# The causal mask of the narrow score units, moved from a TensorE product to a VectorE addition

## The chip, the cores and the metric

One Trainium2 chip, one of its cores. The metric is the device time of one execution in microseconds. Within the core five engines run from queues of their own: TensorE (PE, with its weight loads shown as PEld), VectorE (DVE), ScalarE (ACT), GpSimd (POOL) and SyncE (SP, which only issues DMAs here). They wait for one another on semaphores. Each queue is worked off strictly in its written order.

## The reference

The kernel computes one transformer layer with adaptive layer norm on x of shape 2 x 1024 x 128, in float32. What matters here is the attention; behind it stand a router with the two best of eight experts for each token and a shared expert.

```python
h = _layernorm(x) * (1 + ca) + sa
c_q, c_kv = h @ W_dq, h @ W_dkv
Q = (c_q @ W_uq).reshape(2, 1024, 16, 8)       # K, V likewise from c_kv
scores = jnp.einsum('bqhd,bkhd->bhqk', Q, K) / math.sqrt(8)
scores = jnp.where(jnp.tril(jnp.ones((1024, 1024), bool)), scores, -jnp.inf)
attn = jax.nn.softmax(scores, axis=-1)
out = jnp.einsum('bhqk,bkhd->bqhd', attn, V).reshape(2, 1024, 128)
x = x + ga * (out @ W_o)
h = _layernorm(x) * (1 + cb) + sb
x = x + gb * (shared_expert(h) + the two best of eight experts, weighted)
```

## The kernel before

Attention runs as eight tasks, t = 0 to 7: two batches by four groups of four heads. A task has two halves of 512 queries (c = 0, 1) and key blocks j of 128 keys. Three kinds of work belong to a task.

*Max units* (`max_scores`, L1598 to 1613, and `max_unit`, L1221 to 1237). For the softmax the kernel first needs each query's largest score. TensorE forms scores of 128 queries against up to 512 keys in one PSUM bank (`mx`), and VectorE reduces them: a plain reduction (L1235) off the diagonal, a masking reduction (L1231, one instruction a head) on it. The results of a half are gathered (`maxima`, negm, L1244), split in three bfloat16 parts by GpSimd, turned by TensorE (L1621), copied by VectorE (`neg_out`, L1252) and sent by DMA into three extra rows of the query operand. The product of a score unit then holds the score minus the maximum already. There are 38 max units in a task. They, and the turned pieces of other stages, take the banks `mx` 0, 1, 2 in turn: TensorE may fill a bank again only when the unit three places earlier has been read (`ring_free`).

*Score units* (`score_unit`, L1624 to 1649). TensorE forms the scores of 128 keys against the queries from the diagonal on, up to 512 columns in a bank (`sc`). SCORE lists the 38 units of a task. Where the queries left of a half are at most 256 wide, a unit packs two heads (256 columns each) or four (128 columns each) in one bank. So the units with more than one head are, in each task, 8, 9 (two heads) and 10 (four heads) of the first half, and 35, 36 (two) and 37 (four) of the second: the last three of each half, one right after the other. All other diagonal units hold one head. On the diagonal (22 of the 38 units) a further product, identity times `after`, adds -3e38 where the key is later than the query (L1646 to 1649); `after` holds four copies of the 128 x 128 triangle in bfloat16, and one product covers the first 128 columns of each head of the unit. ScalarE then takes the exponential of the unit in one instruction (`exps`, L894). The banks `sc` 0, 1, 2 go round too: score unit g waits for the exponential of unit g - 3 (four banks near the end of the last task).

*Weighing* (`weigh`, L1652 to 1667). TensorE multiplies the exponentials `pr` with the values, four heads side by side on the array, in float32, into `oacc`. Weighing of two key blocks at a time (of one in the first and last task) is placed when the score units are three units past them (LAG; four in the last task). At the end of a half ScalarE copies `oacc` out (L903), TensorE turns it (L1674) and VectorE divides (L1267, L1269).

The order is written out by `attention_order`, and all engines walk the same list. Max units run ahead of the score units: at first 20, then three for each of the first ten score units, and from there one max unit after each score unit, so that score unit k of task t is followed by max unit k + 2 of task t + 1. After the last max unit of a half its turning is due five max units later. `BETWEEN` and `LATE` put other work into the list: the gates (VectorE L1114 to 1126) in task 1, the row modulations in task 3, the projection and the routing of finished tokens in tasks 4, 5 and 7, and the lists of expert tiles (`tile_list`, L1304 on) at score units 3, 5, 7, 9 of task 7. VectorE has in this list the max units, the copies and the routing, but no work on score units. The experts follow the attention and begin when all weighing is done (`up_copy`, L1350).

The lines which the change touches:

```python
act.wait_ge(s["score_ready"], g + 1)                       # exps
elif kind == "score" and t == T - 1 and k in FIRST_LIST:   # VectorE's walk
if diagonal:                                               # score_unit
```

Of the kernel before, what the change touches and what calls it, by code (L numbers as in the profile page):

```python
# [13 lines left out]
ALU = mybir.AluOpType  # L14
# [7 lines left out]
P = 128  # L22
# [41 lines left out]
SCORE = score_units()  # L64
NM = len(MAXU)
NU = len(SCORE)
# [33 lines left out]
FIRST_LIST = (3, 5, 7, 9)  # L100
# [100 lines left out]
    return held, prior, turned, lent  # L201


def span(g, h):

    return (4 * g + 2 * h, 2) if g == 3 else (4 * g, 4)


def adaln_layer(nc, x, cT, wmod, wdqT, wdkvT, wuq, wuk, wuv, wo, wr1, br1, wr2, br2,
# [18 lines left out]
    for kind, t, k in ORDER:  # L228
        if kind == "out" and k == 0:
            task = t  # L230
        elif (kind, t, k) in SPARE_BANK:
            LENT[kind, t, k] = task
            BACK[task + 1] = (kind, t, k)
    FREED = {x: n + 1 for units in (BY_ACT, BY_DVE) for n, x in enumerate(units)}
    DIAGONAL = [(t, k) for t in range(T) for k in range(NM) if MAXU[k][6]]
    RING = 3
    NLOAD = 9
# [10 lines left out]
    with ExitStack() as ctx:  # L248
# [3 lines left out]
        def sem(name):  # L252
# [139 lines left out]
            xt_ready xt_done up_w down_w hid_ready y_done  # L392
            const_ready pad_ready chain_v chain_p chain_a cs_ready csb_ready comp_ready wqkv_ready mod_ready mod_done r1b_ready ones_ready
            var_ready std_ready xn_ready xT_ready hT_ready qk_ready hi_ready r1_ready mid_ready lo_ready
            v_ready v_done aux_ready aux_free negm_ready neg3_ready score_ready exp_done
            vb_ready pv_done o_done var2_ready
            xn2_ready gx_ready up_ready dn_ready acc_done y_ready wog_ready
            act_free rowm_ready gs_ready""".split()
# [413 lines left out]
        def _(act):  # L812
# [71 lines left out]
            def exps(t, k):  # L884

                c, j, h, n, q0, w, _ = SCORE[k]
                g = NU * t + k
                group = NG * t + GROUPS.index((c, j))
                if h == 0 and group >= NBUF:
                    act.wait_ge(s["pv_done"], group - NBUF + 1)  # L890
                act.wait_ge(s["score_ready"], g + 1)
                src = score_bank(g)[:, 0:n * w].rearrange("p (h n) -> p h n", h=n)
                at = q0 - HALF * c
                act.activation(pr[:, group % NBUF, h:h + n, at:at + w], src, ACT.Exp,  # L894
                               scale=float(DK) ** -0.5).then_inc(s["exp_done"], 1)
# [127 lines left out]
        def _(dve):  # L1023
# [197 lines left out]
            def max_unit(t, k, a):  # L1221
# [14 lines left out]
                        "p (h n) -> p h n", h=n), AX_X, ALU.max)  # L1236
                ins.then_inc(s["aux_free"], 1)

            def maxima(t, c):

                dve.wait_ge(*freed(("max", t, LAST_MAX[c])))
                if t >= 1:
                    dve.wait_ge(s["neg3_ready"], 2 * t + c - 1)
                dve.tensor_reduce(negm[:, c, :], mxp[:, c, :, :, :].rearrange("p k h i -> p (h i) k"), AX_X, ALU.max,  # L1244
                                  negate=True).then_inc(s["negm_ready"], 1)
# [138 lines left out]
            for kind, t, k in ORDER:  # L1384
                a = PLACE.get((kind, t, k))
                if (kind, t, k) in ON_ACT:
                    continue
                if kind == "max":
                    max_unit(t, k, a)
                    if k in LAST_MAX:  # L1390
                        maxima(t, LAST_MAX.index(k))
                    for g, step in norms:
                        if step < 2:
                            second_stats(g, step)
                        else:
                            second_var(g)
                    norms = [(g, step + 1) for g, step in norms if step < 2]
                    for g, step in bests:
                        if step == 0:
                            best_two(g)  # L1400
                        elif step < 3:
                            best_index(g, step - 1)
                        else:
                            choose(g)
                    bests = [(g, step + 1) for g, step in bests if step < 3]
                elif kind == "turn":
                    neg_out(t, k, a)
                elif kind == "mod":
                    mod_out(a)
                elif kind == "gates":  # L1410
                    gates_out(a)
                elif kind == "rowmod":
                    rowmod_out(a)
                elif kind == "at":
                    attn_turned(t, a)
                elif kind == "wo":
                    second_x(t, k, a)
                    if t < 2:
                        norms.append((t, 0))
                    elif t == 3 and k == 0:  # L1420
                        second_stats(t, 0)
                    elif t == 3:
                        second_stats(t, 1)
                        second_var(t)
                    else:
                        second_stats(t, 0)
                        second_stats(t, 1)
                        second_var(t)
                        second_rstd(t)
                elif kind == "x2t":  # L1430
                    hidden_turned(t, a)
                elif kind == "rt":
                    router_relu(t, k, a)
                elif kind == "lg":
                    logits_out(t, k, a)
                    if t < 2:
                        bests.append((t, 0))
                    elif t == 3:
                        best_two(t, k)
                        best_index(t, k)  # L1440
                    else:
                        best_two(t)
                        best_index(t, 0)
                        best_index(t, 1)
                        choose(t)
                elif kind == "pf":
                    slots_of(t, a)
                elif kind == "list":
                    tile_list(t, k)
                elif kind == "score" and t == T - 1 and k in FIRST_LIST:  # L1450
                    tile_list(0, FIRST_LIST.index(k))
                elif kind == "pick":
                    choose(t)
                elif kind == "root":
                    second_rstd(t, 1 if k else 2)
                elif kind == "begin":
                    experts.append(expert(0))
                    up_copy(0)
                elif kind == "half":
                    half_out(k, a)  # L1460
                elif kind == "first":
                    experts.append(expert(1))
                    up_copy(1)
                    down_copy(0)
                elif kind == "out":
                    attn_out(t, k, a)
                elif kind == "head":
                    if t + 2 < ROUTED:
                        experts.append(expert(t + 2))
                        up_copy(t + 2)  # L1470
                    if t + 1 < ROUTED:
                        down_copy(t + 1)
                elif kind == "down" and k == 3:
                    shared_out(t, a)
                elif kind == "odds":
                    gate_sums()
                elif kind == "tail":
                    y_out(t)
# [24 lines left out]
        def _(pe):  # L1503
# [120 lines left out]
            def score_unit(t, k):  # L1624
# [15 lines left out]
                for m in range(n):  # L1640
# [2 lines left out]
                    ins = pe.matmul(dst[:, w * m:w * m + w], S3[0:CROSS + 3, r3, 0, kk:kk + P],  # L1643
                                    S3[0:CROSS + 3, r3, 1, q:q + w], start=(m == 0), stop=True,
                                    skip_group_check=(m > 0))
                if diagonal:  # L1646

                    ins = pe.matmul(dst[:, 0:n * w].rearrange("p (h n) -> p h n", h=n)[:, :, 0:P], identb[:, :],  # L1648
                                    after[:, 0:n, :], start=False, stop=True, skip_group_check=True)
# [260 lines left out]
```

## Time and profile before

| | |
|---|---|
| time, median of 3 runs | 447.58 us (446.93 to 448.43) |
| span of the profiled execution | 445.2 us |
| PE busy | 397.4 us, 89% |
| PE weight loads busy | 231.8 us, 52% |
| DVE busy | 326.0 us, 73% |
| ACT busy | 265.9 us, 60% |
| POOL busy | 142.9 us, 32% |
| mean granted TensorE clock | 0.969 of full speed |

The page gives no time for the profiled execution beside its span; the span is 2.4 us less than the median. Attention's score units lie between 46 and 308 us, the experts between 309 and 421 us. Two things must be kept in mind in reading a timeline. A matmul's duration includes its way through the array, and the next one starts before it ends: what it costs in a row of matmuls is the distance from its start to the next start. The same holds, in a smaller measure, for VectorE, where a reduction's record lasts 0.68 us and the next begins after 0.61 us.

### The profile page before, as it was taken

To read this page: it belongs to the slowest core of one execution; us is meant where nothing else is said; L and a number is where in the kernel's file an instruction comes from. 1 tells how busy PE (TensorE), PEld (TensorE's weight loads), DVE (VectorE), ACT (ScalarE), POOL (GpSimd) and SP (SyncE) were. 2 spreads that over 40 slices of the span, in tenths; PEclk is the share of its full clock that TensorE was granted. 3 is DMA by queue.
4 is the path that set the end of the run, shared out by engine and by line. 5 is a ranking of instruction groups with operands and counts; after the bars stand their busy time and mean duration, and the time that the engine had idled before them with its cause. 6 is when DMAs were issued, how large, how long until landed. Compare 5 with 4: busy or idle time off the path is not lost.

```text
span 445.2 us, 9323 instructions
## 1 busy us (share of the span) xinstructions
PE 397.4 (89%) x2901; PEld 231.8 (52%) x2901; DVE 326.0 (73%) x1187; ACT 265.9 (60%) x609; POOL 142.9 (32%) x237
## 2 busy tenths in 40 slices
PE   6679889989999999999989899999989999999900
PEld 3335433443443543545533443434767889999900
DVE  5747799888888887889796887735687665555527
ACT  3623647647666766667665566787756755555632
POOL 2520350000010020105576333504177575334410
PEclk9959999999999999999999999999999999999975
DMA  5433321044040120210210000493012233210153
GB/s 151 144 112 109 94 58 54 1 104 148 1 110 1 35 77 0 67 45 0 68 45 18 21 21 18 116 315 70 7 54 67 73 91 95 68 36 27 37 194 102
DMA packets 28819, 31.77 MB, mean 71 GB/s; under 512 B 4851, under 2 KB 23387, under 8 KB 28267
## 3 DMA queue, kind: packets, MB, share of 16 engines
q1 hardware_dynamic: 26067, 26.12, 21.1%
q0 software_dynamic: 2272, 4.67, 3.1%
q8 instruction: 23, 0.38, 0.4%
q10 hardware_dynamic: 432, 0.39, 0.3%
q14 instruction: 25, 0.20, 0.2%
HBM read 21.04 MB, written 9.85 MB: 69 GB/s over the span
## 4 chain that ended last, share of the span: by engine, by line
PE 69%; DVE 14%; issue 5%; DMA 5%; ACT 3%; POOL 2%; SPq 1%; DVEq 0%; ACTq 0%; POOLq 0%
PE oacc L1665 14%; PE mx L1612 12%; PE sc L1643 11%; PE sc L1798 6%; PE oacc L1811 6%; DVE mxp L1235 3%; DVE masked L1231 3%; PE sc L1648 2%; PE sc L1818 2%; PE mx L1765 2%; PE mx L1674 2%; ACT osb L903 2%; POOL slot_rows L734 2%; PE mx L1754 1%; DMA parts<-token_results 1%
## 5 line engine op out<-in xcount | busy, mean ns | idle before, releaser
L894 ACT ACTIVATE pr<-sc 128x512 f32<-128x512 f32 (+1 forms) x296 | 154.0, 579 | 87.3 <-PE sc L1648 47.6
L1612 PE MATMUL mx<-S 72*128 72x512 bf16 (+3 forms) x384 | 112.8, 331 | 13.6 <-DMA S<-q_parts 6.1
L1231 DVE CUSTOM_DVE_ANT_0 masked<-mx,later 128x128 f32<-128x128 f32 (+3 forms) x256 | 111.6, 485 | 17.0 <-PE mx L1612 16.1
L1643 PE MATMUL sc<-S 75*128 75x512 bf16 (+3 forms) x373 | 108.1, 328 | 0.0
L1235 DVE TENSOR_REDUCE mxp<-mx 128x1 f32<-128x512 f32 x128 | 82.5, 684 | 20.9 <-PE mx L1612 20.5
L1665 PE MATMUL oacc<-pr,vb 128*32 128x512 f32 (+3 forms) x768 | 73.9, 493 | 0.0
L1612 PEld LDWEIGHTS mx<-S 72*128 72x128 bf16 x384 | 34.7, 99 | 52.2 <-DVE mxp L1231 14.8
L958 ACT ACTIVATE pr<-sc,bcur 128x128 f32<-128x128 f32 x156 | 44.6, 369 | 26.6 <-PE sc L1798 26.5
L1643 PEld LDWEIGHTS sc<-S 75*128 75x128 bf16 x373 | 34.5, 97 | 46.4 <-issue 21.2
L740 POOL DMA_INDIRECT token_results<-S,xrow x39 | 39.1, 1003 | 48.0 <-DVE S L1372 44.6
L654 POOL CAST neg<-negm 128x16 bf16<-128x16 f32 x16 | 3.2, 198 | 139.7 <-DVE negm L1244 139.7
L1798 PE MATMUL sc<-xTg,vb 128*128 128x128 f32 x312 | 41.6, 276 | 2.6 <-ACT xTg L950 2.5
L1811 PEld LDWEIGHTS oacc<-vb,pr 128*128 128x128 f32 x312 | 39.0, 192 | 7.2 <-issue 6.0
L1648 PE MATMUL sc<-after,identb 128*128 128x128 bf16 (+2 forms) x172 | 41.9, 244 | 0.0
L1811 PE MATMUL oacc<-vb,pr 128*128 128x128 f32 x312 | 41.3, 275 | 0.3 <-ACT pr L958 0.3
L734 POOL DMA_INDIRECT slot_rows<-parts,rowi x32 | 31.6, 986 | 30.2 <-PE sc L1648 13.6
L1798 PEld LDWEIGHTS sc<-xTg,vb 128*128 128x128 f32 x312 | 37.9, 192 | 3.6 <-ACT xTg L950 3.3
L1665 PEld LDWEIGHTS oacc<-pr,vb 128*32 128x32 f32 x768 | 19.0, 108 | 31.1 <-issue 15.9
L1357 DVE COPY vb<-S 128x512 f32 x39 | 18.4, 472 | 20.8 <-issue 11.3
L1372 DVE TENSOR_TENSOR S<-oacc,be_sb 128x128 f32<-128x128 f32 x39 | 11.3, 290 | 18.0 <-PE oacc L1811 16.4
L1231 DVE DVE_READ_ACCUMULATOR2_ANT mxp<- 128x1 f32 x256 | 21.0, 82 | 0.0
L1648 PEld LDWEIGHTS sc<-after,identb 128*128 128x128 bf16 x172 | 16.8, 98 | 7.4
(279 smaller groups left out, 471.2 us busy)
## 6 DMA issues: line engine op xcount, KB each, us to landing
S<-q_parts SPq DMA_DIRECT2D x48, 96.0 KB
S<-k_parts SPq DMA_DIRECT2D x21, 192.0 KB
xrow<-slot_rows SPq DMA_DIRECT2D x39, 64.5 KB, 1.8
S<-in_we SPq DMA_DIRECT2D x1, 2048.0 KB, 9.1
S<-in_we SPq DMA_DIRECT2D x4, 512.0 KB, 9.9
parts<-token_results SPq DMA_DIRECT2D x4, 512.0 KB, 5.7
x_sb<-in_x SPq DMA_DIRECT2D x4, 256.0 KB, 4.0
out_y<-attn SPq DMA_DIRECT2D x4, 256.0 KB, 2.3
```

What stands on the lines that cost most here:

```text
L734: pool.indirect_dma_start(xd, bass.IndirectOffsetOnAxis(ap=rowi[:, g, k, n:n + 1], axis=0), rowsk[:, g % 2, n, k, :], None).then_inc(sent[ ...
L740: pool.indirect_dma_start(yd, bass.IndirectOffsetOnAxis(ap=xrow[:, i % XR, C:C + 1].bitcast(I32), axis=0), yst[:, i % ROWS, :], None).then ...
L894: act.activation(pr[:, group % NBUF, h:h + n, at:at + w], src, ACT.Exp, scale=float(DK) ** -0.5).then_inc(s["exp_done"], 1)
L958: ins = act.activation(hid[:, i % 2, P * f:P * f + P], sc[:, i % 2, P * f:P * f + P], ACT.Silu, bias=bcur[:, i % FREE, f:f + 1])
L1231: ins = dve.tensor_tensor_reduce(masked[:, d % 2, w * m:w * m + w], unit[a][:, w * m:w * m + w], later[:, HALF - w:HALF], 1.0, LOWEST, ALU ...
L1235: ins = dve.tensor_reduce(mxp[:, c, place, h:h + n, i - 4 * c], unit[a][:, 0:n * w].rearrange("p (h n) -> p h n", h=n), AX_X, ALU.max)
L1612: ins = pe.matmul(dst[:, w * m:w * m + w], S3[0:CROSS, r3, 1, q:q + P], S3[0:CROSS, r3, 0, kk:kk + w], start=(m == 0), stop=True, skip_gro ...
L1643: ins = pe.matmul(dst[:, w * m:w * m + w], S3[0:CROSS + 3, r3, 0, kk:kk + P], S3[0:CROSS + 3, r3, 1, q:q + w], start=(m == 0), stop=True, ...
L1648: ins = pe.matmul(dst[:, 0:n * w].rearrange("p (h n) -> p h n", h=n)[:, :, 0:P], identb[:, :], after[:, 0:n, :], start=False, stop=True, s ...
L1665: ins = pe.matmul(oacc[VW * h:VW * h + VW, c, at:HALF], vb[:, t % 2, j, h, :], pr[:, group % NBUF, h, at:HALF], start=(j == 0), stop=(j == ...
L1798: ins = pe.matmul(sc[:, i % 2, P * f:P * f + P], wcur[:, i % 2, P * f:P * f + P], xTg[:, i % 2, :], start=True, stop=True)
L1811: ins = pe.matmul(oacc[:, i % 2, 0:P], hid[:, i % 2, P * f:P * f + P], wcur[:, i % 2, FF + C * f:FF + C * f + C], start=(f == 0), stop=(f ...
```

## The change

A new helper names the units: task 1 or later, diagonal, more than one head. These are six units in each of seven tasks, 42 in all. For them TensorE leaves its mask product out and signals after the score products. VectorE, at the unit's place in the common list (before the max unit that follows it there, and before a piece of `tile_list`), waits for the signal and adds `after` in place to the first 128 columns of each head (`blot`), and ScalarE's exponential waits for that addition instead of the product. The semaphore `blot_done` counts the additions. Everything else, task 0 included, stays.

```diff
+def masked_by_dve(t, k):
+    return t >= 1 and SCORE[k][6] and SCORE[k][3] > 1
...
+    BLOTTED = [(t, k) for t in range(T) for k in range(NU) if masked_by_dve(t, k)]
...
     # ScalarE, exps
-                act.wait_ge(s["score_ready"], g + 1)
+                if masked_by_dve(t, k):
+                    act.wait_ge(s["blot_done"], BLOTTED.index((t, k)) + 1)
+                else:
+                    act.wait_ge(s["score_ready"], g + 1)
...
     # VectorE
+            def blot(t, k):
+                _, _, _, n, _, w, _ = SCORE[k]
+                g = NU * t + k
+                dve.wait_ge(s["score_ready"], g + 1)
+                corner = score_bank(g)[:, 0:n * w].rearrange("p (h n) -> p h n", h=n)[:, :, 0:P]
+                dve.tensor_tensor(corner, corner, after[:, 0:n, :], ALU.add).then_inc(s["blot_done"], 1)
...
-                elif kind == "score" and t == T - 1 and k in FIRST_LIST:
-                    tile_list(0, FIRST_LIST.index(k))
+                elif kind == "score":
+                    if masked_by_dve(t, k):
+                        blot(t, k)
+                    if t == T - 1 and k in FIRST_LIST:
+                        tile_list(0, FIRST_LIST.index(k))
...
     # TensorE, score_unit
-                if diagonal:
+                if diagonal and not masked_by_dve(t, k):
```

## Rows read from the trace of the kernel before

**Rows 1.** The page: busy time by engine, then the chain that ended last.

```profile
PE 397.4 (89%) x2901; PEld 231.8 (52%) x2901; DVE 326.0 (73%) x1187; ACT 265.9 (60%) x609; POOL 142.9 (32%) x237
...
PE 69%; DVE 14%; issue 5%; DMA 5%; ACT 3%; POOL 2%; SPq 1%; DVEq 0%; ACTq 0%; POOLq 0%
```

**Rows 2.** Windows: stretch, its length, then busy PE, PEld, DVE, ACT, POOL.

```profile
100.00:280.00 180.00, 173.51 (x1311) 79.82 (x1310) 151.21 (x552) 118.19 (x232) 47.84 (x108) 1.00 0.15 42
```

**Rows 3.** Groups by line and shape: busy us, mean ns, idle before.

```profile
L1149 DVE TENSOR_TENSOR x_sb<-oacc,x_sb 128x512 f32<-128x512 f32 x2 | 1.4, 688 | 0.0
L1149 DVE TENSOR_TENSOR x_sb<-mx,x_sb 128x256 f32<-128x256 f32 x2 | 0.8, 408 | 0.0
```

**Rows 4.** Timeline of PE, task 3, end of the second half: start, us, instruction.

```profile
178.53 0.38 PE L1648 MATMUL sc<-after,identb 128*128 128x512 bf16 x1
178.75 0.38 PE L1612 MATMUL mx<-S 72*128 72x256 bf16 x2
...
182.25 0.34 PE L1612 MATMUL mx<-S 72*128 72x384 bf16 x1
```

**Rows 5.** Timeline of DVE, the same stretch, with idle time before in brackets.

```profile
178.54 0.69 DVE L1231 CUSTOM_DVE_ANT_0 masked<-mx,later 128x512 f32<-128x512 f32 x1
...
181.41 0.42 DVE L1231 CUSTOM_DVE_ANT_0 masked<-mx,later 128x256 f32<-128x256 f32 x1 [0.40 <-PE mx L1612]
...
183.95 0.56 DVE L1231 CUSTOM_DVE_ANT_0 masked<-mx,later 128x384 f32<-128x384 f32 x1 [0.68 <-PE mx L1612]
```

**Rows 6.** Timeline of PE and DVE, task 4, end of the first half.

```profile
186.52 0.27 PE L1648 MATMUL sc<-after,identb 128*128 128x256 bf16 x1
186.63 0.38 PE L1612 MATMUL mx<-S 72*128 72x512 bf16 x1
...
190.44 1.29 DVE L1235 TENSOR_REDUCE mxp<-mx 128x1 f32<-128x512 f32 x2 [1.00 <-PE mx L1612]
...
191.19 0.40 PE L1612 MATMUL mx<-S 72*128 72x128 bf16 x4
```

**Rows 7.** Timeline of PE: its waits for DVE in tasks 1 and 5.

```profile
97.86 0.39 PE L1612 MATMUL mx<-S 72*128 72x512 bf16 x1 [1.23 <-DVE gB L1117]
...
226.81 0.40 PE L1612 MATMUL mx<-S 72*128 72x128 bf16 x4 [0.29 <-DVE mxp L1235]
```

**Rows 8.** Timeline of DVE: idle after the narrow units in tasks 3, 4, 5, 6.

```profile
160.79 1.29 DVE L1235 TENSOR_REDUCE mxp<-mx 128x1 f32<-128x512 f32 x2 [0.70 <-PE mx L1612]
...
214.37 0.42 DVE L1231 CUSTOM_DVE_ANT_0 masked<-mx,later 128x256 f32<-128x256 f32 x1 [0.84 <-PE mx L1612]
...
253.09 0.42 DVE L1231 CUSTOM_DVE_ANT_0 masked<-mx,later 128x256 f32<-128x256 f32 x1 [0.34 <-PE mx L1612]
...
262.79 0.69 DVE L1235 TENSOR_REDUCE mxp<-mx 128x1 f32<-128x512 f32 x1 [0.81 <-PE mx L1612]
```

**Rows 9.** Timeline of PE, DVE and ACT: end of task 6, task 7.

```profile
282.76 0.38 PE L1643 MATMUL sc<-S 75*128 75x512 bf16 x1
...
283.40 0.22 DVE L1252 COPY negT<-mx 48x128 bf16<-48x128 bf16 x1 [1.95 <-PE mx L1621]
...
288.51 0.22 DVE L1326 TENSOR_REDUCE tile_e<-past 128x9 f32<-128x72 f32 x1
...
289.58 0.17 DVE L1332 TENSOR_TENSOR at_e<-at_e,took_e 128x8 f32<-128x8 f32 x1
...
291.05 0.39 PE L1643 MATMUL mx<-S 75*128 75x512 bf16 x1
...
307.28 0.74 DVE L1197 TENSOR_SCALAR parts<-mx,br_sb 32x512 f32<-32x512 f32 x1 [2.15 <-PE mx L1733]
...
307.89 0.60 ACT L894 ACTIVATE pr<-sc 128x512 f32<-128x512 f32 x1 [0.77 <-PE sc L1648]
```

**Rows 10.** Timeline of DVE: the shortest 512 wide operation, and a stretched one.

```profile
95.93 0.43 DVE L1115 TENSOR_SCALAR attn<-attn 128x512 f32<-128x512 f32 x1
...
232.27 1.25 DVE L1296 SCALAR_TENSOR_TENSOR rowi<-place 128x8 int32<-128x8 f32 x1
```

More of the change, by code:

```diff
@@ L394, in adaln_layer @@
             var_ready std_ready xn_ready xT_ready hT_ready qk_ready hi_ready r1_ready mid_ready lo_ready
-            v_ready v_done aux_ready aux_free negm_ready neg3_ready score_ready exp_done
+            v_ready v_done aux_ready aux_free negm_ready neg3_ready score_ready blot_done exp_done
             vb_ready pv_done o_done var2_ready
```

## The prediction

> **What bounds the kernel now.** I read the page first: TensorE is busy for 89% of the span and holds 69% of the chain that ended last, VectorE 14% [rows 1]. Then one row of the windows over 100 to 280 us, six tasks of steady work: PE 173.5 us of 180, DVE 151.2, ACT 118.2 [rows 2]. TensorE is short of time there, and VectorE, idle for 28.8 us, is not far behind. The row hides where that idle time lies, and on this the change depends. So I read the timelines of PE and DVE around the units that the change touches. They come in runs of three: units 8, 9, 10 (call it run A of a task) and 35, 36, 37 (run B), in tasks 1 to 7, so fourteen runs. The reader is to see two things. TensorE's starts follow one another without a gap, so a product taken away is time for it. And at these runs VectorE is behind TensorE: at 178.54 it begins a reduction and works on without a pause until 181.01, and the pause that ends there is 0.40 us [rows 5], while TensorE began its last max unit before the weighing at 178.75 [rows 4]. TensorE's max unit at 182.25 can start only because VectorE has just read the bank of the one begun at 181.41 (0.69 us of work, to 182.10) [rows 4, 5]: there the engine that ends last is VectorE. After a run comes the weighing, some 1.6 us of TensorE without a max unit, in which VectorE catches up and then idles; that pause is what can absorb more work.
>
> **What the change takes off TensorE.** One mask product of a two-head unit costs the distance of two starts, 186.52 to 186.63, 0.11 us; of a four-head unit 178.53 to 178.75, 0.22 us [rows 4, 6]; the records last 0.27 and 0.38 us, which is depth, not cost. A run holds two and one: 0.44 us. Fourteen runs: 6.2 us. The identity's weight loads go too; they lay under the products before.
>
> **What it puts on VectorE.** No row shows an addition that reads and writes PSUM. The nearest are the additions of a PSUM bank to SBUF, 688 ns for 512 columns and 408 ns for 256 [rows 3]. Two 512 wide reductions in a row take 1.29 us where one takes 0.68 [rows 6], so the next starts 0.61 us on, 0.07 to 0.08 less than the record. I take 0.61 and 0.34 us: 1.29, say 1.28 us a run, 17.9 us over fourteen runs. Bounds: below, the 512 wide operation that lasts 0.43 us [rows 10] and half of it for 256, 0.86 us a run; above, a small operation stretched to 1.25 us by something else [rows 10], which, once in a run, makes it 1.9 us. The nearest rows are of the same operation and width, so I stay with them.
>
> By the Trainium skill's page "VectorE: DVE Perf Modes", section on the TRN2 errata, an operation with a PSUM source costs 120 + FD cycles at 0.96 GHz. That is an estimate of 0.66 and 0.39 us, 1.44 us a run, where the rows give 1.28; by the page the total below would be some 2 us higher.
>
> **What waits behind it.** VectorE does the addition in the list's order, so after the max units it is behind with, and on its own queue the next max unit, the negated maxima and the turned pieces stand behind it. ScalarE's exponential of the unit waits for it; TensorE's score unit three later waits for the exponential (0.5 to 0.6 us), and the max unit three later for VectorE. Both reach TensorE.
>
> *Run B, task 3.* Insert 0.34 before the max unit at 178.54, 0.34 before the next, 0.61 before the one after. VectorE's next unit then starts not at 181.41 but at 181.01 + 1.28 = 182.3, 0.88 later, as 0.40 of the 1.28 went into the pause [rows 5]. TensorE's max unit at 182.25 waits for its bank and had some 0.1 of slack: it moves to 183.0, 0.75 later [rows 4]. The other path: the addition of unit 37 ends about 181.5 and its exponential at 182.2, and then the score unit three later can start, ahead of the max unit that VectorE holds until 183.0: this path is just under the first. The 0.44 us that TensorE saves in the run come ahead of both waits and are lost in them. Afterwards VectorE has its pause of 0.68 us at 183.95 again, as both engines are late by the same, so the delay stays and does not grow.
>
> *Run A, task 4.* The pause behind it is 1.00 us [rows 6]. 1.28 less 1.00 leaves 0.28; the max unit at 191.19 has 0.1 of slack: 0.2 us. Again TensorE's 0.44 is spent waiting; the score unit that needs unit 10's exponential comes 0.1 late.
>
> *All runs*, by the same step (1.28 less VectorE's next pause, less 0.1 where TensorE has it):
> - A of tasks 2 and 4: 0.2 each. A3: pause 0.70 [rows 8]: 0.5. A6: pause 0.81 [rows 8]: 0.4.
> - A1 and A5: VectorE works on without a pause on the gates and on the routing, and TensorE already waits for it, 1.23 and 0.29 us [rows 7]. Nothing absorbs: 1.2 each.
> - B1, B2, B3: 0.75 each. B4: pause 0.84: 0.35. B5: pause 0.34: 0.85 [rows 8].
> - B6: no max units are left, VectorE idles 1.95 us before 283.40, from 281.45 [rows 9]. Only the path by the exponentials counts: with the additions VectorE is done with unit 37 at 281.45 + 1.28 = 282.7, the exponential ends 283.3, and the third score unit of task 7 starts then instead of at 282.76 [rows 9]: 0.5 us.
> - A7: unit 9's addition stands before a piece of the tile list and unit 10's behind it; the piece takes 288.51 to 289.75 [rows 9]. With two additions of 0.34 ahead of the piece, unit 10's runs from 290.4 to 291.1, its exponential to 291.7, and the score unit that takes its bank, four on, starts then instead of at 291.05 [rows 9]: 0.7.
> - B7: unit 37's addition stands behind a routing copy that lasts from 307.28 to 308.0, and takes 0.65: the exponential starts at 308.7, not 307.89 [rows 9]. Its weighing is the last of the attention. Some 0.2 of the 0.8 lies under the weighing of the blocks before it, queued ahead: 0.6 (an estimate). The experts start after it.
>
> Sum: runs A 1.2 + 0.2 + 0.5 + 0.2 + 1.2 + 0.4 + 0.7 = 4.4 us; runs B 2.25 + 0.35 + 0.85 + 0.5 + 0.6 = 4.6 us. In all +9.0 us, with TensorE's savings already in it. Attention's end shifts the experts as a whole. Against the span: 445.2 + 9.0 = 454.2. The median of the runs lies 2.4 us above that span, so 447.6 + 9.0 = 456.6 us. With 0.86 us a run instead of 1.28 each run gives some 0.4 less, 3 us after all; with 1.9 some 0.6 more each, 17. The exponential path sets in at 0.86 as well, so the low end is nearer 3 to 4.
>
> **The rivals.**
> *TensorE keeps its gain.* If VectorE's idle time did take all additions (17.9 us against 28.8 us in 180), each run would shorten by 0.44 us: 447.6 - 6.2 = 441.4 us. For it speaks TensorE's share [rows 1, 2]. Against it: the idle time is not at the runs; it decides only where the pause after a run exceeds 1.28 + 0.44, and only B6 has such a one [rows 9], the rest 0.34 to 1.00. A half of it, additions absorbed and TensorE's gain lost, would be no change, 447.6: for that the priced 1.28 would have to be under the pauses, true of none but B6.
> *The exponentials end last and cost more.* Three banks hold the score units. If the hand-over from TensorE to VectorE to ScalarE takes 0.2 us more than the rows of handed-over work show (starts within 0.1 us of the end before), or VectorE's copy of the negated maxima comes late and its DMA holds the next half, each of twelve runs costs some 0.4 more: 447.6 + 9.0 + 5 = 461.6. For it: three hand-overs in a row where there was one. Against: ScalarE is idle for a third of the time [rows 2] and starts at once.
> *A delay is given back in part.* Where TensorE is held by VectorE anyway (A1, A5, B5), a late run can meet slack that I can't see, for instance the 1.25 us operation [rows 10] that runs behind A5 and may not be stretched at another moment. Then 3 to 5 us of the nine remain: 452.
>
> **How the numbers follow.** My forecast, a loss of 7 to 12 us: 0.50. Given back in part, 450 to 454.5: 0.22. Exponentials on top, above 459.5: 0.12. Within 0.3% (about 1.3 us, what a measurement can tell from nothing) of 447.6 or slightly off: 0.07. TensorE keeps a gain: 0.09. Slower by over 0.3%, 0.84; the same 0.07; faster 0.09. The time is 456.6; the range 450.0 to 461.5 leaves the two ends outside.
>
> **What would show each step.** L1648 drops by 42 products; the new addition's line shows 42 instructions, 28 of about 410 and 14 of about 690 ns. In 100 to 280 us and its longer successor DVE busy grows by 15 us and PE's does not fall by as much as its work. VectorE's pauses behind the runs B vanish or shrink to 0.1, PE's waits for `mxp` (weight loads of L1612) grow, and ScalarE waits for the addition. The distance from one run B to the next in tasks 2 and 3 grows by 0.9 to 1.0 us. The stretch after the attention keeps its length. I am wrong if that distance falls, if VectorE's pauses behind the runs stay as they are, or if the additions last well under 0.4 us.

## The result, and the profile after

The changed kernel takes 461.6 us (median) against 448.4 us of the kernel before in the same comparison; the ratio is 1.027, with a 95% interval of 1.023 to 1.031. That is 12.0 us slower (10.3 to 13.7). Forecast were 9.0 us more, 456.6 us, and a range of 450.0 to 461.5. The direction came out, the size was 3 us short, and the median lies 0.1 us above the top of the range; the ratio times the forecast's own base of 447.6 gives 459.6. One of the five executions of the changed kernel, 469.9 us, was in the chip's slower state and is not in the ratio. The profiled execution's span is 457.2 us, 12.0 more than before; its time, 459.0 us, is the lowest of the five.

The page first: busy time, then TensorE's granted clock in forty slices (9 is nine tenths of full speed or more), then the chain that ended last.

```profile
PE 402.4 (88%) x2859; PEld 228.9 (50%) x2859; DVE 342.6 (75%) x1229; ACT 265.6 (58%) x609; POOL 142.7 (31%) x237
...
PEclk9979999989999999999998799999999999999975
...
PE 55%; DVE 24%; issue 9%; DMA 5%; ACT 4%; POOL 2%; SPq 1%; DVEq 1%; ACTq 0%; POOLq 0%
```

The same row of clocks in the kernel before:

```profile
PEclk9959999999999999999999999999999999999975
```

TensorE has 42 products fewer and its share of the chain falls from 69% to 55%; VectorE's rises from 14% to 24% [rows 1]. VectorE is busy for 16.6 us more. One thing the prediction did not have: slices of the attention in which the clock of TensorE is below full speed (the ninth, and the 22nd and 23rd). The groups by line and shape (busy us, mean ns, idle before) give the price of an addition and who waits now:

```profile
L1254 DVE TENSOR_TENSOR sc<-sc,after 128x256 f32<-128x256 f32 x28 | 11.7, 425 | 1.0 <-PE sc L1663 0.9
L1254 DVE TENSOR_TENSOR sc<-sc,after 128x512 f32<-128x512 f32 x13 | 9.0, 689 | 0.0
L903 ACT ACTIVATE pr<-sc 128x512 f32<-128x512 f32 x234 | 126.7, 604 | 90.8 <-DVE sc L1254 41.2 <-PE sc L1663 25.9 <-PE sc L1668 23.2
L1632 PEld LDWEIGHTS mx<-S 72*128 72x128 bf16 x384 | 34.5, 98 | 54.4 <-DVE mxp L1240 17.4 <-DVE mxp L1244 9.2 <-issue 8.5
L1663 PEld LDWEIGHTS sc<-S 75*128 75x128 bf16 x373 | 35.0, 98 | 57.3 <-ACT pr L903 25.9 <-issue 20.0
```

425 and 689 ns are close to what the nearest rows said (408 and 688) [rows 3]. ScalarE waits 41.2 us for the additions, most of it in place of waits for TensorE: in the kernel before its idle time ahead of these exponentials was 78.8 us, here it is 90.8. The distance from one run B to the next, forecast to grow by 0.9 to 1.0 us, grows by 0.91 and 0.93 (marks below). Now the place that the prediction worked out, the end of task 3's second half, by engine, DVE first, then ACT, then PE (start, us, instruction, idle before):

```profile
181.17 0.43 DVE L1254 TENSOR_TENSOR sc<-sc,after 128x256 f32<-128x256 f32 x1
181.51 0.68 DVE L1240 CUSTOM_DVE_ANT_0 masked<-mx,later 128x512 f32<-128x512 f32 x1
...
182.34 0.42 DVE L1254 TENSOR_TENSOR sc<-sc,after 128x256 f32<-128x256 f32 x1
...
183.50 0.69 DVE L1254 TENSOR_TENSOR sc<-sc,after 128x512 f32<-128x512 f32 x1
184.11 0.41 DVE L1240 CUSTOM_DVE_ANT_0 masked<-mx,later 128x256 f32<-128x256 f32 x1
...
187.32 0.56 DVE L1240 CUSTOM_DVE_ANT_0 masked<-mx,later 128x384 f32<-128x384 f32 x1 [0.68 <-PE mx L1632]
```

```profile
184.29 2.07 ACT L903 ACTIVATE pr<-sc 128x512 f32<-128x512 f32 x4 [0.91 <-DVE sc L1254]
```

```profile
184.94 0.39 PE L1663 MATMUL sc<-S 75*128 75x512 bf16 x1 [0.56 <-ACT pr L903]
...
185.62 0.34 PE L1632 MATMUL mx<-S 72*128 72x384 bf16 x1
```

The next instruction starts 0.34 us after an addition of 256 columns begins and 0.61 after one of 512. (From the 120 + FD cycles at 0.96 GHz of the Trainium skill, "VectorE: DVE Perf Modes", section on the TRN2 errata, the estimate is 0.39 and 0.66 us; from start to start the trace has 0.05 less, and it decides.) The pause of 0.40 us [rows 5] is gone, and the one of 0.68 is back unchanged behind the run. TensorE waits 0.56 us for the exponential of unit 37. Behind that the weight load of the max unit at 185.62 waits another 0.20 for VectorE. So here the path by the exponential, which the prediction had just under the other, takes the larger part of the delay.

A good ruler for such a kernel is the row of ScalarE's copies of `oacc` at the end of each half: sixteen marks, found by filtering the timeline of ACT. The marks of tasks 2 and 3 (A2, B2, A3, B3), before and then after:

```profile
133.04 0.59 ACT L903 ACTIVATE osb<-oacc 128x512 f32<-128x512 f32 x1
...
153.74 0.59 ACT L903 ACTIVATE osb<-oacc 128x512 f32<-128x512 f32 x1
...
163.58 0.59 ACT L903 ACTIVATE osb<-oacc 128x512 f32<-128x512 f32 x1
...
184.28 0.59 ACT L903 ACTIVATE osb<-oacc 128x512 f32<-128x512 f32 x1
```

```profile
134.73 0.59 ACT L912 ACTIVATE osb<-oacc 128x512 f32<-128x512 f32 x1
...
156.18 0.59 ACT L912 ACTIVATE osb<-oacc 128x512 f32<-128x512 f32 x1
...
166.21 0.59 ACT L912 ACTIVATE osb<-oacc 128x512 f32<-128x512 f32 x1
...
187.65 0.59 ACT L912 ACTIVATE osb<-oacc 128x512 f32<-128x512 f32 x1
```

The marks are 1.69, 2.44, 2.63 and 3.37 us later. What a mark's delay adds to the delay of the mark before it is its *step*, the cost of one run of three units: 0.75 for B2, 0.19 for A3, 0.74 for B3. Where the clock does nothing they repeat from profile to profile of a kernel within some 0.02 us, far finer than the time of a kernel can be told, and they are the measure in what follows.

### The profile page after: what moved, and what is told of

Same layout as the page of the kernel before. It is cut to its first block, busy times and chain, and to the rows that moved or that the text cites. A ratio compares the mean times of both kernels' runs of the same rounds, so it can differ in the third digit from the quotient of the medians.

```text
span 457.2 us, 9282 instructions
## 1 busy us (share of the span) xinstructions
PE 402.4 (88%) x2859; PEld 228.9 (50%) x2859; DVE 342.6 (75%) x1229; ACT 265.6 (58%) x609; POOL 142.7 (31%) x237
## 4 chain that ended last, share of the span: by engine, by line
PE 55%; DVE 24%; issue 9%; DMA 5%; ACT 4%; POOL 2%; SPq 1%; DVEq 1%; ACTq 0%; POOLq 0%
PE oacc L1685 11%; PE mx L1632 8%; PE sc L1663 8%; DVE masked L1240 7%; PE sc L1818 6%; PE oacc L1831 5%; DVE mxp L1244 3%; DVE sc L1254 3%; PE mx L1785 2%; PE sc L1838 2%; POOL slot_rows L740 2%; ACT pr L903 2%; PE mx L1694 1%; PE mx L1774 1%; ACT osb L912 1%
## 5 line engine op out<-in xcount | busy, mean ns | idle before, releaser
L903 ACT ACTIVATE pr<-sc 128x512 f32<-128x512 f32 (+1 forms) x296 | 154.0, 581 | 99.3 <-DVE sc L1254 41.2
L1632 PE MATMUL mx<-S 72*128 72x512 bf16 (+3 forms) x384 | 113.3, 333 | 14.4 <-DMA S<-q_parts 6.5
L1240 DVE CUSTOM_DVE_ANT_0 masked<-mx,later 128x128 f32<-128x128 f32 (+3 forms) x256 | 112.2, 484 | 14.4 <-PE mx L1632 13.4
L1663 PE MATMUL sc<-S 75*128 75x512 bf16 (+3 forms) x373 | 109.8, 332 | 4.1 <-ACT pr L903 4.0
L1685 PE MATMUL oacc<-pr,vb 128*32 128x512 f32 (+3 forms) x768 | 79.8, 525 | 0.6 <-ACT pr L903 0.6
L1668 PE MATMUL sc<-after,identb 128*128 128x128 bf16 (+2 forms) x131 | 29.3, 224 | 0.0
L1254 DVE TENSOR_TENSOR sc<-sc,after 128x256 f32<-128x256 f32 (+1 forms) x41 | 20.6, 509 | 1.0 <-PE sc L1663 0.9
```

The lines of the kernel that those rows point to most:

```text
L1240: ins = dve.tensor_tensor_reduce(masked[:, d % 2, w * m:w * m + w], unit[a][:, w * m:w * m + w], later[:, HALF - w:HALF], 1.0, LOWEST, ALU ...
L1254: dve.tensor_tensor(corner, corner, after[:, 0:n, :], ALU.add).then_inc(s["blot_done"], 1)
L1632: ins = pe.matmul(dst[:, w * m:w * m + w], S3[0:CROSS, r3, 1, q:q + P], S3[0:CROSS, r3, 0, kk:kk + w], start=(m == 0), stop=True, skip_gro ...
L1685: ins = pe.matmul(oacc[VW * h:VW * h + VW, c, at:HALF], vb[:, t % 2, j, h, :], pr[:, group % NBUF, h, at:HALF], start=(j == 0), stop=(j == ...
```

## The experiments

Three theories. *V*: VectorE's queue ends last at the runs; its additional work reaches TensorE less the next pause. *H*: the hand-over from TensorE to VectorE to ScalarE costs by itself. *C*: TensorE's granted clock falls, and that is the part beyond the forecast. Where three marks are shown, they are B2, A3 and B3 of that profile, to be compared with the steps 0.75, 0.19, 0.74 of the change. Steps are always against the first profile of the kernel before. The experiments ran on several chips: for the first four, and for all from "only the second halves" on, the kernel before took 462.2 us and not 448. Ratios are always against it on the same chip, and the changed kernel itself was not timed where it takes 462.2.

**TensorE keeps its products too.** VectorE adds zeros (`nought`), and the exponential waits for that.

```diff
-                dve.tensor_tensor(corner, corner, after[:, 0:n, :], ALU.add).then_inc(s["blot_done"], 1)
+                dve.tensor_tensor(corner, corner, nought[:, 0:n, :], ALU.add).then_inc(s["blot_done"], 1)
...
-                if diagonal and not masked_by_dve(t, k):
+                if diagonal:
```

> TensorE keeps its mask product in the 42 units, and VectorE still adds a tile of the same size (zeros, so that the score stays what it was) which the exponential waits for. Tells what TensorE's 6.2 us of saved products were worth. Theory V (VectorE's queue ends last at the runs, the saving is lost in its waits): within 0.3% to at most 1.5 us above the changed kernel, so 11 to 14 us over the kernel before. Rival P (the saving was realised and hides a larger loss): 5 to 6 us above the changed kernel, 17 to 18 over before. Theory C (TensorE's granted clock fell because it had less to do): TensorE is busier here, fewer stretches at half clock than the four of the changed kernel, and the time may even be below it.

Ratio 1.020 (1.017 to 1.024) against the kernel before, 9.3 us, under the 11 to 14 expected; as the changed kernel has no time on that chip, the marks decide.

```profile
161.04 0.59 ACT L913 ACTIVATE osb<-oacc 128x512 f32<-128x512 f32 x1
...
171.07 0.59 ACT L913 ACTIVATE osb<-oacc 128x512 f32<-128x512 f32 x1
...
192.52 0.59 ACT L913 ACTIVATE osb<-oacc 128x512 f32<-128x512 f32 x1
```

From mark to mark 10.03 and 21.45 us, as in the changed kernel (10.03 and 21.44), where TensorE does 0.44 us less in each. What TensorE saves is worth nothing in the ordinary tasks (2 and 3, and run A of task 4) while VectorE adds; it is worth 0.1 us in A7 (1.18 here against 1.08) and 0.2 in B7 (0.57 against 0.34). Theory C's guess, that a busier TensorE keeps its clock, fell: over 103 to 119 us the granted clock is 0.68 here, 10 us at the lower level.

**The products left out, no mask at all.** VectorE's additions go too, and the exponential of these units runs on a thousandth of the score so that it stays finite; this kernel leaves the mask out.

```diff
-                if masked_by_dve(t, k):
-                    act.wait_ge(s["blot_done"], BLOTTED.index((t, k)) + 1)
-                else:
-                    act.wait_ge(s["score_ready"], g + 1)
+                act.wait_ge(s["score_ready"], g + 1)
...
-                dve.wait_ge(s["score_ready"], g + 1)
-                corner = score_bank(g)[:, 0:n * w].rearrange("p (h n) -> p h n", h=n)[:, :, 0:P]
-                dve.tensor_tensor(corner, corner, after[:, 0:n, :], ALU.add).then_inc(s["blot_done"], 1)
```

> The 42 mask products are left out and nobody adds the mask (these units are not masked; their exponential runs with a thousandth of the scale so that it stays finite). The most that the change can give. If TensorE ends last at the runs: 5 to 6 us below the kernel before. If VectorE holds TensorE there (theory V): 1 to 3 us below, as only the second pieces without max units and the exponential path gain.

Ratio 0.999 (0.997 to 1.001): no gain that the time shows, less than the 1 to 3 us that theory V expected.

```profile
153.70 0.59 ACT L909 ACTIVATE osb<-oacc 128x512 f32<-128x512 f32 x1
...
163.28 0.59 ACT L909 ACTIVATE osb<-oacc 128x512 f32<-128x512 f32 x1
...
183.92 0.59 ACT L909 ACTIVATE osb<-oacc 128x512 f32<-128x512 f32 x1
```

Steps -0.26 for A3 (-0.36 for A2 and A4) and -0.06 for B2 and B3. In the second halves of tasks 1 to 3 six sevenths of TensorE's 0.44 us are lost even without any addition, as VectorE ends last there anyway; in the first halves of tasks 2 to 4 most of it is won, and in A7 and B7, with -0.44 each, all of it. From A1 to B4 this is 1.35 us. Behind it this profile, of an execution of 468.6 us, lies at half clock in tasks 5 and 6 (steps B5 5.60, A6 3.91) and loses it all again.

**Load alone.** VectorE adds from SBUF to SBUF, for nobody, and waits for nothing but its own addition before; TensorE masks, ScalarE waits for TensorE.

```diff
-                dve.wait_ge(s["score_ready"], g + 1)
-                corner = score_bank(g)[:, 0:n * w].rearrange("p (h n) -> p h n", h=n)[:, :, 0:P]
-                dve.tensor_tensor(corner, corner, after[:, 0:n, :], ALU.add).then_inc(s["blot_done"], 1)
+                if (t, k) != BLOTTED[0]:
+                    dve.wait_ge(s["blot_done"], BLOTTED.index((t, k)))
+                dve.tensor_tensor(idle[:, :].bitcast(BF16)[:, 0:n * P], later[:, 0:n * P],
+                                  after[:, 0:n, :].rearrange("p h n -> p (h n)"), ALU.add).then_inc(s["blot_done"], 1)
```

> As the kernel before, TensorE masks, the exponential waits for TensorE; but VectorE does 42 additions of the same width at the same places of its queue, from SBUF to SBUF, for which nobody waits. Theory V: 5 to 9 us over the kernel before, most of the loss. Theory H (the hand-over TensorE to VectorE to ScalarE makes it): under 2 us over.

Ratio 1.017 (1.013 to 1.022).

```profile
162.44 0.59 ACT L909 ACTIVATE osb<-oacc 128x512 f32<-128x512 f32 x1
...
172.48 0.59 ACT L909 ACTIVATE osb<-oacc 128x512 f32<-128x512 f32 x1
...
193.95 0.59 ACT L909 ACTIVATE osb<-oacc 128x512 f32<-128x512 f32 x1
```

Steps 0.77, 0.20 and 0.77. The load by itself makes the whole step of the ordinary tasks, and the additions' content, their PSUM bank and the saved products make none. It does not make the steps of B4 (0.01), A7 (0.00) and B7 (-0.06), and of B6 only 0.43.

**Hand-over alone.** TensorE masks; ScalarE waits for a count of VectorE, which waits for the unit and does nothing else.

```diff
-                dve.tensor_tensor(corner, corner, after[:, 0:n, :], ALU.add).then_inc(s["blot_done"], 1)
+                dve.sem_inc(s["blot_done"], 1)
```

> As the kernel before, TensorE masks; but the exponential of the 42 units waits for a semaphore that VectorE counts up at the unit's place in its queue, after it waited for the score unit, without any addition. Theory H: 4 us or more over the kernel before. Theory V: under 2 us over: the wait in VectorE's order costs only where VectorE is far behind (first run of task 1, task 5).

Ratio 1.008 (1.005 to 1.010), 3.6 us.

```profile
155.58 0.59 ACT L912 ACTIVATE osb<-oacc 128x512 f32<-128x512 f32 x1
...
165.42 0.59 ACT L912 ACTIVATE osb<-oacc 128x512 f32<-128x512 f32 x1
...
186.12 0.59 ACT L912 ACTIVATE osb<-oacc 128x512 f32<-128x512 f32 x1
```

Steps 0.00, 0.00, 0.00, and in all tasks only A5 0.42 and A7 0.32, the two places where small routing operations stand in VectorE's queue, and B5 3.25, of which more below. So V, and not H. The time lies between what the two theories expected (under 2 us, 4 or more) and does not tell them apart: 1.8 us were lost before the first hand-over and some behind the attention, so they are no effect of the hand-over that I can show.

**The kernel before again, on a chip on which it takes 447.8 us.**

> The kernel before, unchanged, for its profile on the chip of this call: a chip on which it took 462.2 us was met in the call before, against 447.6 on the chip of the first comparison. Theory C (TensorE's granted clock makes the difference between chips and between runs): more stretches at half clock than the one at 21 to 31 us that the first profile of it has, where the time is above 450. If the time is 447 to 450, no further stretch.

It ran once, in 449.0 us; its span is 447.3, 2.1 more than the first profile's. Busy time and clock of the stretch of task 5, first profile, then this one (PE, PEld, DVE, ACT, POOL, clock):

```profile
228.00:256.00 28.00, 24.58 (x180) 10.86 (x181) 21.81 (x88) 16.32 (x32) 15.86 (x22) 1.00 0.05 16
```

```profile
228.00:256.00 28.00, 25.30 (x145) 10.54 (x144) 19.28 (x75) 14.30 (x28) 14.04 (x19) 0.82 0.04 14
```

Theory C's bound was wrong: at 449 us the kernel before has time at half clock too, by the clock of 0.82 some 10 us of the 28. Its step B5 is 3.46 us with no addition anywhere. The first profile, on which the prediction rested, was one without it.

**The changed kernel again.**

> The changed kernel, unchanged, on the same chip as the others of this call. Theory V with the sum of the prediction (9.0 us): ratio 1.020. Theory C on top, as in the first profile (17 us at half clock within the attention): ratio 1.025 to 1.03, and its profile has more time at half clock within the attention than the kernel before on this chip.

Four times between 457.9 and 473.1 us against 447.8, too far apart for a ratio. Steps of its profile: A1 2.14 and B1 5.78, and then 0.17, 0.75, 0.19, 0.75, 0.17, 0.60 up to B4, the same as in the first but for A1 and B1. The profile is of an execution of 470.2 us; behind B4 it differs from the first in A5 (1.72) and B5 (5.44), and behind the attention by 2.3 us.

**Without A1, A5, B5.**

```diff
-    return t >= 1 and SCORE[k][6] and SCORE[k][3] > 1
+    return t >= 1 and SCORE[k][6] and SCORE[k][3] > 1 and t != 5 and (t, k > 10) != (1, False)
```

> The change without the three runs of units that meet a VectorE without a pause: first half of task 1, both halves of task 5; there TensorE masks as before. 33 of 42 additions stay. By the prediction's sum these three make 3.25 of 9.0 us, so 5.7 us over the kernel before remain (ratio 1.013). Theory C: in the first profile the same three runs held 1.7 + 3.6 + 1.4 us, more than the sum says, and all stretches at half clock; then 5 us or less remain and the stretches within the attention are as few as in the kernel before.

Ratio 1.023 (1.018 to 1.028), no less than the 1.027 of the change by these intervals. The steps A1 and A5 are 0.00, B5 is 3.48 as in the kernel before again, the others as in the changed kernel; without B5 they sum to 5.9 us, where the prediction's sum had 5.7. The three steps went, but the time did not follow: beside B5 the profile is 3.8 us longer behind the attention, with 3 us at half clock between 320 and 360 us. The claim that these three runs hold all of the half clock is wrong.

**Only the first halves, only the second halves.**

```diff
+    return t >= 1 and SCORE[k][6] and SCORE[k][3] > 1 and k < 11
...
+    return t >= 1 and SCORE[k][6] and SCORE[k][3] > 1 and k > 11
```

> Only the first-half units (8, 9, 10) of tasks 1 to 7 are masked by VectorE, 21 of 42. By the prediction's sum 4.4 us over the kernel before (ratio 1.010), of which 3.1 in tasks 1, 5 and 7. Theory H (hand-over) has no reason for a difference between tasks: 0.6 us in each.

Ratio 1.029 (1.023 to 1.036) by the times, far above the 1.010 expected, though the profiled execution's span is only 6.6 us over the 447.3 of the kernel before on the same chip.

> Only the second-half units (35, 36, 37) of tasks 1 to 7 are masked by VectorE. Theory V: steps of 0.75 us in tasks 1, 2, 3, 0.6 in task 4, 0.7 in task 6, and no step in the first halves; in all 3.5 to 4 us over the kernel before plus what the clock does in task 5. Theory C: no half clock near 98 to 118 us, as the first half of task 1 has no addition.

Ratio 1.011 (1.007 to 1.014). Step for step the two kernels add up to the change, but for A3 and A7, which are larger where the second halves have no additions, and B5, which lies at half clock in both (3.47 and 4.27). The first has 1.48, 0.17, 0.46, 0.17, 1.30, 0.35, 1.40 in A1 to A7 and zero in all B but B5; the second 0.75, 0.75, 0.76, 0.60 in B1 to B4, 0.73, 0.35 in B6, B7 and zero in all A.

**Only where the pause is longer than the load.** Units 8 and 9 (0.68 us) and 35 (0.34 us), tasks 2, 3, 4, 6.

```diff
+    return t in (2, 3, 4, 6) and k in (8, 9, 35)
```

> VectorE masks only where its next pause is longer than what it gets: units 8, 9 (0.68 us) and 35 (0.34 us), in tasks 2, 3, 4 and 6; 12 additions, the other units as in the kernel before. Pauses there: 0.7 to 1.0 us behind the first halves, 0.40 and 0.84 behind the second halves of tasks 2, 3 and of task 4. Theory V: the loss turns into a small gain, from one end of half to the next, 0.1 to 0.2 us less in the first halves (two products of 0.11 us saved) and 0 to 0.1 less in the second; in all 0.5 to 1.0 us below the kernel before, under what its time can show, so the steps in the profile decide. Theory H (hand-over costs by itself): a third to a half of the loss per task of the changed kernel stays, 0.3 to 0.4 us a task.

Ratio 0.997 (0.995 to 1.000).

```profile
154.20 0.59 ACT L912 ACTIVATE osb<-oacc 128x512 f32<-128x512 f32 x1
...
163.82 0.59 ACT L912 ACTIVATE osb<-oacc 128x512 f32<-128x512 f32 x1
...
184.52 0.59 ACT L912 ACTIVATE osb<-oacc 128x512 f32<-128x512 f32 x1
```

Steps 0.00 for B2, -0.22 for A3 (9.62 us instead of 9.84) and 0.00 for B3; -0.22 in A2 and A4 and -0.12 in A6. In tasks 2 to 4 the two saved products of 0.11 us of a first half arrive whole, in task 6 half of them. In the second halves the load of 0.34 is below the pause too (0.40 and 0.84), and there the loss becomes nothing and not a gain, as the saved product is lost there even without an addition. In all it is 0.8 us, a version ahead of both kernels by its steps and not surely by its time.

**The load of A1 alone.** The load experiment for units 8, 9, 10 of task 1 only.

```diff
+    return t == 1 and k in (8, 9, 10)
```

> The kernel before, but with three additions of VectorE from SBUF to SBUF, for which nobody waits, at the places of units 8, 9, 10 of task 1: 1.3 us of VectorE, once. Theory V alone: TensorE 1.3 to 1.5 us later behind task 1's first half and no more after it. Theory C: the granted clock falls to half somewhere in 95 to 120 us for 3 to 14 us, which no profile without additions there shows, and in some executions some 5 us are added by it.

Ratio 1.012 (1.007 to 1.018). The stretch 103 to 119 us, in which there is no addition, of the kernel before and then of this one:

```profile
103.00:119.00 16.00, 15.84 (x109) 6.78 (x111) 13.59 (x38) 12.11 (x25) 0.00 (x0) 1.00 0.28 100
```

```profile
103.00:119.00 16.00, 16.00 (x69) 5.96 (x69) 9.57 (x33) 7.70 (x15) 0.00 (x0) 0.58 0.28 99
```

A granted clock of 0.58 over 16 us means 13.4 us at the lower of the two levels, 1.2 GHz, and TensorE starts 69 matmuls in place of 109. Step A1 is 2.15, B1, without any addition, 5.02, and all later ones but B5 (1.44) are zero. 1.3 us of VectorE's time cost 7 us here. Just before, TensorE waited (timeline of PE, idle in brackets). The first of these waits the kernel before has too [rows 7], the other two it has not:

```profile
97.83 0.39 PE L1630 MATMUL mx<-S 72*128 72x512 bf16 x1 [1.23 <-DVE gB L1123]
...
100.80 0.39 PE L1630 MATMUL mx<-S 72*128 72x512 bf16 x1 [0.18 <-DVE mxp L1241]
...
102.08 0.22 PE L1639 MATMUL mx<-identb,neg 128*48 128x128 bf16 x1 [0.68 <-DVE mxp L1241]
```

**A1 with the first wait filled.**

```diff
-                for m in range(n):
+                for m in [m for _ in range(6 if (t, k) == (1, 10) else 1) for m in range(n)]:
```

> The changed kernel, but TensorE forms the products of unit 10 of task 1 six times instead of once (the last one counts), 1.1 us of matmuls at the place where it otherwise waits 1.2 us for VectorE. Theory C: the clock stays at full speed in 95 to 120 us, the step of the first half of task 1 is 1.5 us and that of its second half 0.75, and the time is at or below that of the changed kernel on the same chip. If the clock falls there all the same, what TensorE does just before is not its cause.

Ratio 1.044 (1.039 to 1.049), slower than any other. The matmuls shorten the wait before the max unit from 1.67 us, in both profiles of the changed kernel, to 0.56; the later waits stay:

```profile
100.67 0.39 PE L1663 MATMUL sc<-S 75*128 75x512 bf16 x1 [0.42 <-ACT pr L903]
...
101.93 0.39 PE L1663 MATMUL sc<-S 75*128 75x512 bf16 x1 [0.65 <-ACT pr L903]
```

```profile
103.00:119.00 16.00, 16.00 (x70) 6.04 (x71) 9.62 (x32) 8.14 (x16) 0.00 (x0) 0.59 0.28 99
```

The clock falls all the same. Filling that one wait is no cure. As the waits between 100 and 103 us are still there, it does not settle which of them matters. In the first profile of the changed kernel the clock fell earlier, right behind the wait that is filled here: the weighing that follows it takes 3.11 us where the kernel before takes 1.71.

```profile
97.14 0.39 PE L1632 MATMUL mx<-S 72*128 72x512 bf16 x1 [1.67 <-DVE gB L1126]
97.46 3.11 PE L1685 MATMUL oacc<-pr,vb 128*32 128x512 f32 x16
```

## Why the prediction was right, and where it was short

Steps in us, forecast and in the first profile of the change (for B5 the 3.46 of the kernel before again is taken off):

| | A1 | A2 | A3 | A4 | A5 | A6 | A7 | B1 | B2 | B3 | B4 | B5 | B6 | B7 | sum |
|---|---|---|---|---|---|---|---|---|---|---|---|---|---|---|---|
| forecast | 1.2 | 0.2 | 0.5 | 0.2 | 1.2 | 0.4 | 0.7 | 0.75 | 0.75 | 0.75 | 0.35 | 0.85 | 0.5 | 0.6 | 9.0 |
| measured | 1.51 | 0.16 | 0.19 | 0.17 | 1.30 | 0.36 | 1.08 | 0.75 | 0.75 | 0.74 | 0.59 | 0.17 | 0.72 | 0.34 | 8.8 |

*The mechanism was right at the ordinary runs.* "There the engine that ends last is VectorE": the load alone gives the steps, the hand-over alone gives none, and the rule "1.28 less VectorE's next pause, less 0.1" hit A2, A4, A6 and B1 to B3 within 0.05 us.

*The price of an addition was right*: 0.34 and 0.61 us.

*That the 0.44 us which TensorE saves in a run are lost: shown* by the kernel that does both, within 0.02 us in the steps A2 to B4; only in A7 and B7 are 0.1 and 0.2 us kept. The rival that TensorE keeps its gain is out.

*Single terms were off.* A3 was forecast at 0.5 and is 0.19 in the change, but 0.46 where only the first halves have additions: the run before it takes the 0.3 away, and how is open. At A7 load alone gives 0.00 and the hand-over alone 0.32, so the 1.08 needs both: ScalarE's exponential is late by VectorE's tile list and the addition, as forecast, and more of it stays. Without additions in the second halves A7 is even 1.40. At B4 the load alone gives 0.01 and the change 0.59: I looked at VectorE's pause of 0.84, and the delay went through ScalarE, whose copy of the turned tokens stands behind the late exponentials; TensorE's routing product waits 0.31 us for that copy:

```profile
219.13 1.02 PE L1753 MATMUL oacc<-hT,wr_sb 128*32 128x512 f32 x2 [0.31 <-ACT hT L937]
```

At B6 TensorE waits 0.50 and 0.21 us for the exponentials, the path that the prediction named, with 0.7 in place of 0.5. But it is not the only path there: the load alone, for which no exponential waits, gives 0.43. B5 lies in a stretch at half clock, and its own share can't be told: 0.17 by the change, 0.8 by the second halves alone. That the sum of the steps, 8.8, comes so near to the 9.0 is luck in part: A1 (which has 3.4 us at half clock in or beside it), A5, A7, B4 and B6 are 1.25 us over together, A3, B5 and B7 1.25 under.

*What was missing is the clock.* Of the 12.0 us between the two spans 8.8 are the steps and 3.5 the half clock in task 5; -0.7 lie before the first addition and +0.4 behind the attention. The 3.5 us are a difference between executions of the same kernel, for the kernel before has them in its second profile and not in its first. So they explain the two spans, and not yet the ratio, which is taken over several executions of both kernels. Whether the change makes them more frequent isn't settled: the step B5 is 3.2 to 5.4 us in all six profiles with additions in it, and 0 to 3.5 in seven of the eight without, 5.6 in the eighth.

One part of the clock does go with the change. Of fourteen profiles (two of the kernel before) the seven with work put on VectorE in A1 (the changed kernel twice, both, load alone, first halves, load of A1, filled A1) all have 3 to 14 us at half clock between 95 and 119 us; the seven without have none. Both groups have profiles from each of the later chips, and the kernel with the load of A1 differs from the kernel before in nothing else: that work of VectorE there brings the fall is shown. In A1 TensorE waits for VectorE already [rows 7], and the additional waits are what these profiles share. That the waits are the cause is the likely reading, and not shown; the one try to take them away removed only a part of them, and in two profiles the fall comes behind the first wait, in the other five some 5 us later. By its step B1 it costs nothing beyond the 0.75 in the first profile (3.4 us at half clock) and 5.0 us where it lasts 13.4. Between the two profiles of the changed kernel, of executions of 459.0 and 470.2 us, A1 and B1 make 5.7 of the 11.2 us. This is a term that the forecast lacked; how much of the missing 3 us it is, averaged over executions, isn't known.

## What to carry to other kernels

Before work moves from the busier engine to the less busy one, look at where the receiver pauses, not at how long it is idle in all: the cost was the load less the next pause behind it, and where the load was shorter than the pause it was nothing or a small gain. Where two engines hold each other by a ring of buffers, marks that come once in each round, such as the copy at the end of a half, agree within 0.02 us from profile to profile, in a kernel whose times vary by 3 us. A small delay can cost several times its length if TensorE's clock falls behind it: read the granted clock of each stretch before a difference is put down to anything else, and take a second profile of the kernel before.

## What the hardware showed beside that

The same kernel took 447.8 us on one chip and 462.2 on others. The kernel with 12 of the 42 additions, profiled on one of the latter, has nearly the attention steps of the kernel before and its loss behind the attention, in the experts; the kernel before, on the first chip, has full clock there. The kernel before first, then that one (PE, PEld, DVE, ACT, POOL, clock):

```profile
360.00:385.00 25.00, 24.51 (x216) 24.00 (x215) 14.68 (x41) 12.82 (x45) 13.55 (x14) 1.00 0.32 86
```

```profile
360.00:385.00 25.00, 18.65 (x119) 15.78 (x118) 9.29 (x33) 10.03 (x33) 13.01 (x13) 0.80 0.25 71
```

The clock is 0.80 there, and TensorE is busy for 18.7 of 25 us against 24.5. So on that chip TensorE fell to the lower level in a stage that no experiment touched. All eight profiles from the slower chips are 11.0 to 14.5 us longer behind the attention than the first profile of the kernel before; the five others are -0.3 to 3.8 us longer. That is most of the 14.4 us between the chips, though the kernel before itself was not profiled on a slower one. Why the clock falls there on some chips was not tried.
